# Attention stages without the products of the identity that TensorE computes ahead of its waits

## The reference, cut to what matters

```
x = _layernorm(x + _L0_attn_ref(x, Wq, Wk, Wv, Wo, bo))          # stage a: causal self attention, 16 heads of 16
x = _layernorm(x + _L0_xattn_ref(x, ctx, itok, W_kvc, ...))      # stage a: latent cross attention, a key is seen
                                                                 #          within 8 places of the token's id
x = _layernorm(x + _L0_ffn_ref(x, ...))                          # stage b: 16 experts, the 4 best of a token
x = _layernorm(x + _L1_attn_ref(x, ...))                         # stage c: gated delta rule
x = _layernorm(x + _L1_xattn_ref(x, ctx, mask, wq, bq, ...))     # stage d: cross attention, queries and output
                                                                 #          through 8-bit quantised products
x = _layernorm(x + _L1_ffn_ref(x, W_gate, W_qkv))                # stage d: causal attention; of 16 heads of keys
                                                                 #          and values a token gives its best one
```

## Time and profile before

| | us |
|---|---|
| median of 3 runs | 2141.43 (2130.88 to 2142.25) |
| the profiled execution | 2148.16 |
| its span | 2146.4 |
| PE busy in the span | 1955.3 (91%), 10062 matmul records |
| DVE busy | 1415.7 (66%) |
| ACT busy | 920.0 (43%) |
| mean granted clock of PE | 0.944 |

### The profile page before, as it was taken

How to read it: one execution, slowest core, us unless ns; L and a number is a source line. 1 busy time by engine, 2 the same in 40 slices (tenths; PEclk the granted TensorE clock), 3 DMA queues, 4 the chain that set the end, 5 groups by cost and what they waited for, 6 DMA issues and landing times. The chain is left out here.

```text
span 2146.4 us, 27311 instructions
## 1 busy us (share of the span) xinstructions
PE 1955.3 (91%) x10062; PEld 1448.3 (67%) x10062; DVE 1415.7 (66%) x3249; ACT 920.0 (43%) x1691; POOL 78.6 (4%) x103
## 2 busy tenths in 40 slices
PE   6989889899998889998999999999999997999997
PEld 4868678655555558577585775866758666767665
DVE  2767667332322677877878788677886776677776
ACT  3454554211111544344443544444434442564573
POOL 0000000100002000000000000000000001000000
PEclk9999899899998899999999999999999998899998
DMA  4000000400001120211301102021020210100000
GB/s 144 6 11 6 6 1 1 188 1 0 0 1 59 29 59 11 40 41 20 69 12 40 41 16 55 31 40 41 16 55 20 50 20 17 32 12 2 13 6 5
DMA packets 125938, 65.35 MB, mean 30 GB/s; under 512 B 109360, under 2 KB 116080, under 8 KB 124944
## 3 DMA queue, kind: packets, MB, share of 16 engines
q1 hardware_dynamic: 125808, 63.62, 11.7%
HBM read 53.46 MB, written 9.96 MB: 30 GB/s over the span
## 5 line engine op out<-in xcount | busy, mean ns | idle before, releaser
L1408 PE MATMUL c_bank<-c_Y,c_NP 128*128 128x128 f32 x1536 | 189.8, 287 | 0.0
L1408 PEld LDWEIGHTS c_bank<-c_Y,c_NP 128*128 128x128 f32 x1536 | 186.5, 203 | 3.3 <-issue 3.3
L1736 DVE TENSOR_TENSOR c_Y<-c_V,c_bank 128x512 f32<-128x512 f32 x192 | 131.9, 687 | 84.2 <-PE c_bank L1408 84.2
L1332 PE MATMUL c_bank<-c_xT,c_wqk 128*128 128x512 f32 x256 | 118.0, 604 | 8.9 <-ACT c_zs L1561 5.4
L1667 DVE SCALAR_TENSOR_TENSOR c_cv<-c_pad,c_wcv,c_cv 128x1024 f32<-128x1024 f32 x96 | 122.6, 1284 | 4.9 <-ACT c_cv L1543 2.3
L1710 DVE SCALAR_TENSOR_TENSOR c_NP<-c_NP,c_cj,c_bank 128x256 f32<-128x256 f32 x256 | 104.9, 478 | 29.3 <-ACT c_NP L1571 29.3
L1667 DVE SCALAR_TENSOR_TENSOR c_cv<-c_pad,c_wcqk,c_cv 128x1024 f32<-128x1024 f32 x96 | 122.3, 1282 | 2.3 <-ACT c_cv L1543 1.5
L964 ACT ACTIVATE b_sg<-b_G 128x512 f32<-128x512 f32 x50 | 29.7, 597 | 214.6 <-PE b_G L909 214.6
L1485 PE MATMUL c_bank<-c_wout,c_yT 128*128 128x256 f32 x512 | 121.3, 383 | 0.0
L1029 DVE TENSOR_TENSOR b_inner<-b_prod,b_R 128x512 f32<-128x512 f32 x44 | 30.3, 688 | 124.3 <-PE b_R L923 124.3
L1332 PE MATMUL c_bank<-c_xT,c_wv 128*128 128x512 f32 x256 | 111.2, 592 | 0.0
(11 more groups left out here) (410 smaller groups left out, 3926.3 us busy)
## 6 DMA issues: line engine op xcount, KB each, us to landing
b_wup<-b_in_wup SPq DMA_DIRECT2D x4, 1280.0 KB, 14.6
c_wqk<-c_in_wqk SPq DMA_DIRECT2D x9, 512.0 KB, 3.2
c_wv<-c_in_wv SPq DMA_DIRECT2D x8, 512.0 KB, 3.4
c_wz<-c_in_wz SPq DMA_DIRECT2D x8, 512.0 KB, 4.6
c_wout<-c_in_wout SPq DMA_DIRECT2D x8, 512.0 KB, 3.5
diagonal_blocks<-c_NP SPq DMA_DIRECT2D x64, 64.0 KB, 2.0
c_A<-diagonal_blocks SPq DMA_DIRECT2D x8, 512.0 KB, 3.6
c_NP<-no_blocks SPq DMA_DIRECT2D x32, 128.0 KB, 4.4
```

Of the source, the lines that this page charges most:

```text
L1332: last = pe.matmul(four(pair[q][:, :]), w[:, c * P:(c + 1) * P], xT[:, c, 4 * q:4 * q + 4, :], start=c == 0, stop=c == DC - 1)
L1408: last = pe.matmul(banks[n % 4][:, b * P:(b + 1) * P], lhsT(h, 4 * q + b), rhs(h, 4 * q + b), start=True, stop=True)
L1736: dve.tensor_tensor(rr(Y, h, q), rr(V, h, q), four(banks[n % 4][:, :]), ALU.subtract).then_inc(s["y_ready"], 1)
```

## The change

The helper and its seven calls are removed. No wait, no tile and no other instruction changes, and the order of all that is left is the same.

```diff
--- before.py
+++ after.py
@@ -115,12 +115,6 @@
     running = list(programs)
     while running:
         running = [p for p in running if next(p, done) is not done]
-
-
-def keep_busy(pe, times, bank, ident):
-
-    for _ in range(times):
-        pe.matmul(bank[:, 0:2 * P].rearrange("p (a n) -> p a n", a=2), ident, spread(ident, 2), start=True, stop=True)
 
 
 def fill_identity(pool, link, tile):
@@ -427,7 +421,6 @@
                                  start=True, stop=True)
             last.then_inc(products_ready, 1)
             pe.wait_ge(consts, 1)
-            keep_busy(pe, 5, lanes[0].O, ident[:, :])
             pe.wait_ge(weights, 16 * len(now))
             pe.wait_ge(products_copied, 6)
 
@@ -493,8 +486,6 @@
                 last.then_inc(L.y1_ps, 1)
                 yield
                 yield
-                if L.n == 0:
-                    keep_busy(pe, 5, L.S, ident[:, :])
                 pe.wait_ge(L.ln1.done, i + 1)
                 for c in range(DC):
                     last = pe.transpose(L.M[:, c * P:(c + 1) * P], L.x1[:, c * P:(c + 1) * P], ident[:, :])
@@ -517,8 +508,6 @@
                                              start=True, stop=True)
                     last.then_inc(L.Q_ps, 1)
                     yield
-                if L.n == 0:
-                    keep_busy(pe, 2, L.O, ident[:, :])
                 pe.wait_ge(L.seg_step, at(i, 4, 4))
                 seg4 = spread(L.segb[:, :], 4)
 
@@ -2025,8 +2014,6 @@
             def project8(i, L, n, out):
 
                 yield
-                if n:
-                    keep_busy(pe, (4, 3)[L.n], L.S, ident[:, :])
                 pe.wait_ge(L.xquant.done, at(i, 2, n + 1))
                 for c in range(DC):
                     last = pe.transpose(L.Mb[:, c * P:(c + 1) * P], L.x8[:, n, c * P:(c + 1) * P], identb[:, :])
@@ -2064,7 +2051,6 @@
                 yield
                 if i:
                     pe.wait_ge(L.self_att.o_done, at(i - 1, QUADS, QUADS))
-                keep_busy(pe, (4, 2)[L.n], L.O, ident[:, :])
                 pe.wait_ge(L.yb_ready, at(i, 2, 1))
                 for c in range(DC):
                     last = pe.transpose(L.M[:, c * P:(c + 1) * P], L.yb[:, 0, c * P:(c + 1) * P], ident[:, :])
@@ -2093,8 +2079,6 @@
                 yield from project8(i, L, 1, L.M[:, D:2 * D])
                 yield
                 yield
-                if L.n == 0:
-                    keep_busy(pe, 11, L.S, ident[:, :])
                 pe.wait_ge(L.ln1.done, i + 1)
                 for c in range(DC):
                     last = pe.transpose(L.M[:, c * P:(c + 1) * P], L.x5[:, c * P:(c + 1) * P], ident[:, :])
```

## The result

| | before | after |
|---|---|---|
| median, us | 2141.43 (7 runs, 2130.88 to 2148.72) | 2159.96 (7 runs, 2150.98 to 2162.82) |
| ratio | | 1.0085, interval 1.0062 to 1.0109 |
| profiled execution, us | 2148.16 | 2159.96 |
| mean granted clock | 0.944 | 0.923 |

The change makes the kernel slower by 0.85%, 18 us. The prediction was 2155 and slower, range 2139 to 2168. The profiled executions differ by less, 11.8 us, because that of before lay at the upper end of its runs: 101 further runs of before, timed beside the experiments, have mean clocks of 0.945 to 0.956, 0.950 in the middle, and the profiled one has 0.944.

The account below looks back on a forecast made before the run. Prediction: the 64 us of removed PE products fill pauses; without them the clock falls to 1.2 GHz over work PE bounds. Terms sum to +13.6 us; from the median 2141.4 it predicted 2155, range 2139 to 2168.

Parts of the forecast that it names:

- Line 2067, +5.7: Stage d, ahead of cross attention: clock falls in the emptier pause, 1.9 us lost in three later passes, +5.7 us.
- 4.2 was taken: Assumed us of low clock falling on resumed work after a pause, between bounds 2.5 and 6.0; half lost where PE bounds.
- First pass, -0.7: Stage d's first pass, line 2067: the calls delay transposes by 0.75 us and the clock stands without them, -0.7 us.
- Lines 2029 and 2097, +1.0 a pass: Stage d: low clock from end of attention to line 2112's projections, lane 1's projections end 1.0 us later.
- Line 2120, -1.2 a pass: Stage d, krep transposes: products only delay; without them lane 0's scores come 1.3 us earlier, lane 1's 1.15.
- the third rival: Clock falls in line 2120's krep pause too, 1.6 us lost a pass, 6.3 us more, total 2161; chance 0.14.
- Line 497, +8.4: Stage a, ahead of x1's transposes: low clock falls on the following products, 2.1 us lost in four passes, +8.4 us.
- Line 521, 0: Stage a, ahead of cross attention: the two products' 0.87 us is hidden because DVE reads the scores later, 0 us.
- Line 430, +1.0, an even chance: Stage a's opening call: nothing won, even chance of a low stretch after the 3.2 us pause, +1.0 us.
- parts 2 to 4: Stage d's lines 2029, 2097 and 2120 together, four passes: -0.8 us, bounds -4.2 and +2.6.

Follow-up runs that it names:

- e2: The kernel before without the five products at line 2120 alone; 2139.35 us, ratio 0.9997.
- e6: The kernel before without the call at line 497 alone; 2145.15 us, ratio 1.0019.
- e4: The kernel before with only the call at line 2067 kept, the other six out; 2154.73 us, ratio 1.0064.
- e3: The kernel before without stage a's three calls (lines 430, 497, 521); 2152.04 us, ratio 1.0046.
- e7: The kernel before with line 2120's five products ahead of lane 0's krep transpose turned into four ahead of lane 1's; 2138.63 us, ratio 0.9994.
- e1: The kernel before with only the calls at lines 497 and 2067 kept, the other five out; 2146.86 us, ratio 1.0030.

## Why the prediction was right, and where it was not

The mechanism was right: two of the removed calls, 497 and 2067, cover pauses in front of work that PE bounds, and without them this work starts at 1.2 GHz. The sign is right, and 13.6 us against 18.2 lies at the lower edge of the interval (13.3 to 23.3). That the sum comes so near is in part luck: the prediction gave these two calls 13.4 of its 13.6 us, and by their single prices they make 8.6 of 18.2. By the calls:

1. *Line 2067, +5.7, measured 4.5 by the times and 4.8 by the traces.* The level fell in all three passes; 3.0, 4.0 and 5.4 us of it met the scores, 4.1 in the mean where 4.2 was taken. *First pass, -0.7:* wrong in sign in the trace. The clock had not risen yet: stage d's first stretch at 0.50 lasts until 1836.45, and line 2044 to line 2083 takes 13.3 us for 12.3. Before has 1.2 GHz there too, for 6.0 us; the changed kernel has 9.1.
2. *Lines 2029 and 2097, +1.0 a pass:* +4.1 in four. The long low stretch is as described, but against the trace of before it costs only 0.7 us in four passes; the rest is, as far as the traces show, the passes without any low stretch, which the trace of before has not. That the number fits is luck.
3. *Line 2120, -1.2 a pass.* This is the step that failed: -0.6 in all. The delay was there as counted in passes with low clock over line 2112, and 0.4 us in the others. And I let the clock stand behind the new pause and called its fall the third rival, at 0.14. It fell in three passes of the changed kernel and all four of e2. Its price was half of that rival's, 0.8 us a pass instead of 1.6 in e2's first three: the loop was less bound by PE than I allowed. On the rule of the Trainium skill that the prediction cites there (TensorE: Matmul & The Clock Gate, Part 4: PE-mode transpose), that transposes don't count as work for the clock, the runs don't decide, as the pause is thin either way.
4. *Line 497, +8.4, measured 4.1 (interval 0.2 to 7.9).* The mechanism was right, and the traces spread about the size: lines 505 to 540 take 5.1 us more in e6, 5.6 in the changed kernel, 5.7 in e4 and 9.3 in e3 (without the stretch inside its cross attention). Of the low stretches 2.2, 3.6, 5.1 and 2.5 us met lines 505 and 516 in the changed kernel, 3.1 us a pass in e6 and 5.3 in e3, where 4.2 was taken. The 4.2 is in the middle of what happens; by the times the term was twice too high, and what lowered it in the timed runs is not shown.
5. *Line 521, 0:* right for the delay; a low stretch inside the cross attention in one pass of two kernels without the call was not foreseen, and it accounts for little of the 3.6 us measured. The cause of the rest stays open; the interval holds 0.
6. *Line 430, +1.0, an even chance:* the stretch came in every trace without the call and cost about 3 us in four of the five. The even chance had nothing behind it.

The term of line 2120 was too low by 4.2 us and that of line 497 too high by 4.3; they cancel. The terms of lines 521 and 430 were too low by 5.6 us together, and that is what the sum lacks. A slip in the prediction's sum changes nothing: the upper bound of its parts 2 to 4 is +2.8 by its own numbers, not +2.6.

## What to carry to other kernels

Products that fill a pause are worth at most about half of the low-clock time that would fall on work bound by PE behind it, less what they delay: look at what follows the pause, not at the pause, and check whether another engine bounds it. Place them right ahead of the work that is to run at full clock; two in the last pause, added to the eleven in the one before it, did what those alone did in a quarter of the passes. And the mean granted clock is a poor measure of two kernels: the changed one has 0.923 for 0.950, some 120 us more of low clock in an execution (worked out from these means), and is only 18 us slower, and e2 has 0.9465 for 0.949 at the same time. Between executions of one kernel it is a good one: of 101 runs of before, the fastest, 2128.96 us, had 0.956 and the slowest, 2148.24, had 0.947.

## What the runs showed that I had not expected

Savings did not stay: a low stretch came back, or grew, at another place of the same pass: e7 wins 1.35 us at the krep products of passes two to four and loses 1.65 in two of them at the end of the cross attention. And single executions say little. Stages b and c, untouched in all these kernels, took between 1423.0 (e1) and 1432.4 us (e7) in their profiled executions, and the runs of one experiment span 12 to 19 us. Here too it is the clock:

```profile
390.12:1813.13 1423.01, 1313.71 (x6176) 938.12 (x6205) 945.43 (x1897) 557.70 (x826) 62.87 (x61) 0.96 0.15 36
389.99:1822.37 1432.38, 1326.25 (x6204) 949.04 (x6204) 945.35 (x1897) 558.44 (x826) 62.82 (x62) 0.95 0.15 36
```

Summed up, the low stretches in these two stages are 116 us long in e1 and 146 in e7. Over all 14 traces this sum and the length of the stages go together (correlation 0.97, about a third of a us for each us of low clock). A call's price of 3 us can be had only from many runs, or from the steps of the pass that it touches; and even the steps of one trace can mislead, as those of stage d in before did, in which every pass had a low stretch.
